# A scatter that adds: layer 1's expert results summed in device memory, residual rows stored ahead, last loads and stores on two queues

## The reference

```python
x = x + _L0_attn_ref(_layernorm(x), ...)
x = x + _L0_xattn_ref(_layernorm(x), ctx_2048, mask_BxS2_bk0)
x = x + _L0_ffn_ref(_layernorm(x), ...)
x = x + _L1_attn_ref(_layernorm(x), ...)
x = x + _L1_xattn_ref(_layernorm(x), ctx_2048, ctx_2048)
x = x + _L1_ffn_ref(_layernorm(x), ...)
```

```python
scores = jax.nn.softmax(jnp.einsum('bsh,eh->bse', x, router_w) + expert_bias, axis=-1)
top_w, top_idx = jax.lax.top_k(scores, 4)
top_w = top_w / jnp.sum(top_w, axis=-1, keepdims=True)
g = jnp.einsum('bsh,khe->bske', x, gate_proj)
u = jnp.einsum('bsh,khe->bske', x, up_proj)
out = jnp.einsum('bske,keh->bskh', jax.nn.silu(g) * u, down_proj)
sel = jnp.take_along_axis(out, top_idx[..., None], axis=2)
return jnp.sum(sel * top_w[..., None], axis=2)
```

## Time and profile before

| what | us |
|---|---|
| median of 3 runs | 970.37 (970.13 to 981.52) |
| the profiled execution | 980.05 |
| its span, first to last instruction | 978.1 |
| PE busy | 773.2 |
| DVE busy | 552.1 |
| ACT busy | 342.4 |
| POOL busy | 261.8 |
| first instruction of the last stage | 800.5 |
| last scatter of a block's result issued | 955.14 |

### The profile page before, as it was taken

How to read it: one execution, slowest core, us unless ns; L and a number is a source line. 1 busy time by engine, 2 the same in 40 slices (tenths; PEclk the granted TensorE clock), 3 DMA queues, 4 the chain that set the end, 5 groups by cost and what they waited for, 6 DMA issues and landing times. The chain is left out here.

```text
span 978.1 us, 13262 instructions
## 1 busy us (share of the span) xinstructions
PE 773.2 (79%) x4289; PEld 479.4 (49%) x4291; DVE 552.1 (56%) x1333; ACT 342.4 (35%) x781; POOL 261.8 (27%) x334
## 2 busy tenths in 40 slices
PE   4888844999999798994365899988987629999990
PEld 1454423788555465653123555555555315565550
DVE  4888944343232122224648999999986344455445
ACT  2455522333232122221333665666555202222220
POOL 2434314200000000003453334455331421333232
PEclk8999955999999999997566999999979659999995
DMA  9335504280077968663020001110130129999936
GB/s 350 159 157 215 215 1 150 81 318 17 5 274 274 360 221 293 239 236 99 13 63 1 9 15 35 34 47 26 47 135 25 49 85 330 319 325 319 328 117 225
DMA packets 52834, 151.90 MB, mean 155 GB/s; under 512 B 6720, under 2 KB 36288, under 8 KB 47648
## 3 DMA queue, kind: packets, MB, share of 16 engines
q1 hardware_dynamic: 47440, 135.99, 39.1%
q0 software_dynamic: 5328, 15.08, 4.2%
HBM read 109.87 MB, written 41.17 MB: 154 GB/s over the span
## 5 line engine op out<-in xcount | busy, mean ns | idle before, releaser
L1209 PE MATMUL ps<-f_rw,f_xT 128*128 128x512 f32 (+1 forms) x276 | 116.2, 545 | 17.1 <-DMA f_rw<-w_routed 16.5
L1130 DVE TENSOR_TENSOR f_rh<-f_gate,ps 128x256 f32<-128x256 f32 (+1 forms) x69 | 26.0, 377 | 142.8 <-ACT f_gate L1068 82.9
L2023 ACT ACTIVATE b_PX<-ps 128x512 f32<-128x512 f32 x128 | 72.9, 597 | 44.6 <-PE ps L2248 42.4
L1751 DVE TENSOR_REDUCE b_smax<-ps 128x4 f32<-128x1024 f32 x64 | 77.8, 1215 | 15.9 <-PE ps L2224 15.9
L1209 PEld LDWEIGHTS ps<-f_rw,f_xT 128*128 128x128 f32 x276 | 52.2, 194 | 50.4 <-issue 24.9
L2478 POOL DMA_INDIRECT y<-f_ys,f_to x47 | 45.1, 959 | 110.3 <-DVE f_ys L2527 109.3
L1068 ACT ACTIVATE f_gate<-ps 128x256 f32<-128x256 f32 (+1 forms) x69 | 24.0, 348 | 143.8 <-PE ps L1209 143.3
L1501 POOL MEMSET b_half<- 128x1 f32 x1 | 0.1, 98 | 273.6 <-POOLq L64 273.6
L2248 PE MATMUL ps<-b_Q,b_Cx 100*128 100x256 f32 x256 | 57.1, 328 | 10.6 <-ACT b_PX L2023 6.4
L1230 PE MATMUL ps<-f_rw,f_rhT 128*128 128x256 f32 x230 | 60.9, 380 | 0.5 <-ACT f_rhT L1054 0.5
L2224 PE MATMUL ps<-b_Cx,b_Q 96*128 96x512 f32 x128 | 47.5, 454 | 15.5 <-DVE b_smax L1751 9.6
(11 more groups left out here) (318 smaller groups left out, 1752.1 us busy)
## 6 DMA issues: line engine op xcount, KB each, us to landing
f_rw<-w_routed SPq DMA_DIRECT2D x23, 1920.0 KB, 8.0
rows<-a_blank SPq DMA_DIRECT2D x16, 1152.0 KB, 6.8
rw<-w_ffn SPq DMA_DIRECT2D x24, 704.0 KB
f_rw<-w_ffn SPq DMA_DIRECT2D x23, 704.0 KB
f_xs<-rows SPq DMA_DIRECT2D x47, 144.0 KB
f_yk<-y SPq DMA_DIRECT2D x8, 512.0 KB, 7.2
f_raw<-w_shared SPq DMA_DIRECT2D x10, 384.0 KB
b_Cx<-ctx_parts SPq DMA_DIRECT2D x96, 32.0 KB
```

What stands on the lines that cost most here:

```text
L1130: nc.vector.tensor_tensor(rh[u % 2][:, 0:n], gate[u % 2][:, 0:n], ps[:, u % 4, n:2 * n], ALU.mult).then_inc(r_h, 1)
L1209: mm = nc.tensor.matmul(ps[:, u % 4, 0:2 * n], xT[b % 2][:, c, :], rw[b % R_SLOTS][:, off:off + 2 * n], start=(c == 0), stop=(c == C - 1))
L1751: nc.vector.tensor_reduce(smax[t % 2][:, k // C, k % C, :], ps[:, FIRST:FIRST + 2, :].rearrange("p u (g n) -> p (u g) n", g=2), AX, ALU.ma ...
L2023: nc.scalar.activation(PX[g % RING][:].rearrange("p c m -> p (c m)"), ps[:, RETS + G_TURN[g] % 2, :], ACT.Exp, scale=XSC).then_inc(turn_re ...
```

## The change

`y1` is gone. In its place is `sums`, two sums of 1024 + 128 rows in device memory. Blocks with an even number add their rows to the first sum, those with an odd number to the second; the last 128 rows of each take the blank rows.

- In `attention0`, SP fills the rows from 1024 on with zeros (1.31 MB: the first sum's padding and the whole second sum), behind the clearing of `rows0` and ahead of the blank rows of `rows1`, and waits for it at the stage's end.
- In `attention1`, SP stores each tile of `X` into the first sum once `var_ready[2]` has counted it, behind the first weight loads. A row's address is now the token's number alone.
- In `sparse_experts`, the mask product and the reduction handle the weight only. The address comes straight from the loaded row, at most the padding row, plus 1152 for odd blocks; it is computed ahead of the reduction. POOL's scatter adds to what is in device memory. It waits, ahead of the scatter of block b, until that of b − 2, the one before it to the same sum, has landed.
- At the end, SP and ACT each wait for all scatters and load four tiles, 256 KB each with the two sums; DVE adds the two; SP and ACT each store the tiles they loaded. POOL has no part in it.

```diff
@@ attention0, SP
             sp.dma_start(rows_dram.rearrange("(b p) d -> p b d", p=P), bc(empty[:], 1, BLOCKS0)).then_inc(rows_cleared, 16)
+            sp.dma_start(sums_dram[TOKENS:2 * SUM_ROWS].rearrange("(b p) d -> p b d", p=P), bc(empty[:], 1, TILES + 2)
+                         ).then_inc(sums_cleared, 16)
...
             sp.wait_ge(rows_cleared, 16)
+            sp.wait_ge(sums_cleared, 16)
@@ attention1, SP
                 sp.dma_start(rw[n][:], w_ffn[n]).then_inc(w_loaded[n], 16)
+            for t in range(TILES):
+                sp.wait_ge(var_ready[2], t + 1)
+                sp.dma_start(sums_dram[t * P:(t + 1) * P], X[:, t, :]).then_inc(x_stored, 16)
+            sp.wait_ge(x_stored, 16 * TILES)
@@ attention1, DVE
-                nc.vector.tensor_scalar(row[s][:, D + E1:ROW1], rank[s][:], float(TOKENS), K[:, K_TOK + t:K_TOK + t + 1],
-                                        ALU.mult, ALU.add).then_inc(row_ready, 1)
+                nc.vector.tensor_copy(row[s][:, D + E1:ROW1], bc(K[:, K_TOK + t], 1, E1)).then_inc(row_ready, 1)
@@ sparse_experts
+        def take_sums(eng, q):
+
+            for n in range(Y_SLOTS):
+                eng.wait_ge(y_sent[n], 16 * ((BLOCKS1 + Y_SLOTS - 1 - n) // Y_SLOTS))
+            for t in range(q, TILES, 2):
+                eng.dma_start(yk[t][:], parts[t]).then_inc(yk_loaded[t], 16)
+
+        def store_sums(eng, q):
+
+            for t in range(q, TILES, 2):
+                eng.wait_ge(summed, t + 1)
+                eng.dma_start(out[:, t, :], X[:, t, :]).then_inc(stored[q], 16)
+            eng.wait_ge(stored[q], 16 * TILES // 2)
...
-                pool.indirect_dma_start(y_dram, bass.IndirectOffsetOnAxis(ap=to[b % A_SLOTS][:, 0:1], axis=0), ys[b % Y_SLOTS][:], None
-                                        ).then_inc(y_sent[b % Y_SLOTS], 16)
-            for t in range(1, TILES, 2):
-                pool.wait_ge(yk_loaded[t], 16)
-                nc.gpsimd.tensor_tensor(yk[t][:, 0:2], yk[t][:, 0:2], yk[t][:, 2:4], ALU.add).then_inc(odd_sum, 1)
+                if b >= 2:
+                    pool.wait_ge(y_sent[(b - 2) % Y_SLOTS], 16 * ((b - 2) // Y_SLOTS + 1))
+                pool.indirect_dma_start(sums_dram, bass.IndirectOffsetOnAxis(ap=to[b % A_SLOTS][:, 0:1], axis=0), ys[b % Y_SLOTS][:], None,
+                                        compute_op=ALU.add).then_inc(y_sent[b % Y_SLOTS], 16)
...
+                if b >= A_SLOTS:
+                    dve.wait_ge(y_sent[b % Y_SLOTS], 16 * (b // Y_SLOTS))
+                nc.vector.tensor_scalar(to[b % A_SLOTS][:], xs[b % X_SLOTS][:, D + E1:D + E1 + 1], K[:, K_PAD:K_PAD + 1],
+                                        float(b % 2 * SUM_ROWS), ALU.min, ALU.add).then_inc(to_ready, 1)
                 dve.wait_ge(aux_masked, b + 1)
...
+                dve.wait_ge(yk_loaded[t], 16)
+                nc.vector.tensor_tensor(X[:, t, :], yk[t][:, 0], yk[t][:, 1], ALU.add).then_inc(summed, 1)
```

More of the change, by code:

```diff
@@ L97, in decoder_kernel @@
 def decoder_kernel(nc, x, consts, routing, w_attn0, ctx_rows, ctx_cols, ctx_lhs, mask, w_shared0, w_routed0, w_attn1, lam, bias1, w_ffn1,
-                   out, ctx_dram, rows0_dram, y0_dram, rows1_dram, y1_dram):
+                   out, ctx_dram, rows0_dram, y0_dram, rows1_dram, sums_dram):
     with ExitStack() as whole:
@@ L1259, in routed_experts, with attention1 @@
     end_program(nc, semaphores)
-def attention1(nc, w_attn, ctx_lhs, lam, bias, X, K, KR, ps, ctx_dram, y_dram, y_dest, wk, rows_dram, w_ffn, rw, w_loaded, eb, rb, own):
+def attention1(nc, w_attn, ctx_lhs, lam, bias, X, K, KR, ps, ctx_dram, y_dram, y_dest, wk, rows_dram, w_ffn, rw, w_loaded, eb, rb, own,
+               sums_dram):
     ctx = ExitStack()
@@ L1445, in attention1 @@
         prefixed = sem("prefixed")
+        x_stored = sem("x_stored")
         counted = sem("counted")
@@ L2369, in attention1, with sparse_experts @@
     end_program(nc, semaphores)
-def sparse_experts(nc, tag, w_dram, rows_dram, y_dram, X, K, KR, ps, rw, w_loaded, eb, rb, own, out):
+def sparse_experts(nc, tag, w_dram, rows_dram, sums_dram, X, K, KR, ps, rw, w_loaded, eb, rb, own, out):
     ctx = ExitStack()
@@ L2394, in sparse_experts @@
         hT = [sb(f"hT{n}", [P, 2, P]) for n in range(2)]
-        aux = [sb(f"aux{n}", [P, 2, E1]) for n in range(2)]
-        pick = [sb(f"pick{n}", [P, 2]) for n in range(A_SLOTS)]
+        aux = [sb(f"aux{n}", [P, E1]) for n in range(2)]
+        pick = [sb(f"pick{n}", [P, 1]) for n in range(A_SLOTS)]
         to = [sb(f"to{n}", [P, 1], mybir.dt.int32) for n in range(A_SLOTS)]
         ys = [sb(f"ys{n}", [P, D]) for n in range(Y_SLOTS)]
-        nowhere = sb("nowhere", [P, BLOCKS1])
-        yk = [sb(f"yk{t}", [P, TOP1, D]) for t in range(TILES)]
+        yk = [sb(f"yk{t}", [P, 2, D]) for t in range(TILES)]
         xs_loaded = [sem(f"xs_loaded{n}") for n in range(X_SLOTS)]
         h_set = sem("h_set")
-        nowhere_set = sem("nowhere_set")
         x_turned = sem("x_turned")
@@ L2418, in sparse_experts @@
         yk_loaded = [sem(f"yk_loaded{t}") for t in range(TILES)]
[L2419 to L2423, removed]
+        summed = sem("summed")
+        stored = [sem(f"stored{n}") for n in range(2)]
         block = ctx.enter_context(nc.Block())
         ident = K[:, K_ID:K_ID + P]
+        parts = sums_dram.rearrange("(a t p) d -> t p a d", a=2, p=P)
+        def take_sums(eng, q):
[8 more added lines that the diff above has]
+            eng.wait_ge(stored[q], 16 * TILES // 2)
         @block.sync
@@ L2459, in _ @@
                 load_weights(b)
[L2460 to L2468, removed]
+            take_sums(sp, 0)
+            store_sums(sp, 0)
         @block.gpsimd
@@ L2517, in pick_own @@
                 nc.vector.tensor_reduce(pick[b % A_SLOTS][:], aux[b % 2][:], AX, ALU.add).then_inc(picked, 1)
[L2519 to L2523 removed]
             def keep_y(b):
                 dve.wait_ge(down_done, b + 1)
+                dve.wait_ge(picked, b + 1)
                 nc.vector.tensor_scalar(ys[b % Y_SLOTS][:], ps[:, 7, 0:D], pick[b % A_SLOTS][:, 0:1], None, ALU.mult).then_inc(y_kept, 1)
[L2529 to L2531 removed]
             dve.wait_ge(h_set, 1)
@@ L2541, in _ @@
                 pick_own(b)
-                address(b)
                 if b >= 2:
@@ L2707 @@
     rows1 = nc.dram_tensor("rows1", (SPARE1 + 1, P, ROW1), F32).ap()
-    y1 = nc.dram_tensor("y1", (TOP1 * TOKENS + BLOCKS1 * P, D), F32).ap()
-    decoder_kernel(nc, *args, out, ctx_parts, rows0, y0, rows1, y1)
+    sums = nc.dram_tensor("sums", (2 * SUM_ROWS, D), F32).ap()
+    decoder_kernel(nc, *args, out, ctx_parts, rows0, y0, rows1, sums)
     r = _run(nc, [arrays], core_ids=[0])
```

36 lines of the change are left out of this document (11 added, 25 removed).

## The result

| | before | changed |
|---|---|---|
| median of 4 runs, us | 972.75 (970.13 to 981.52) | 991.81 (987.09 to 993.38) |
| ratio, 95% interval | | 1.0172 [1.0095, 1.0249] |
| profiled execution, us | 980.05 | 991.02 |
| its span, us | 978.1 | 989.1 |

The account below looks back on a forecast made before the run. The scatter loop of the expert stage stood at the edge of PE's pace, with a serial end after it. Loop +11.9, last landing +0.4 and end −8.8 gave +3.5 us on 970.37, say 974 us; range 958 to 1012.

Parts of the forecast that it names:

- the rival of the second trip: Expert-stage scatter reads rows, waits, then writes: landing 6.9, block 4.28, together +39 us, 1010 us; chance 0.30.
- scatters 3.3 to 3.6 apart: Sign of being right: spacing in us of scatters in the loaded part of the expert stage.
- the 3.9 that was named as a sign of being wrong: Scatters over 3.9 us apart in the expert stage would show the forecast wrong.
- The loop: Expert-stage scatter loop: (5.2 + 1.66) / 2 = 3.43 us per block against 3.117, over 38 blocks +11.9 us.
- The landing: Adding scatter's time to land: +0.4 us for one more pass of the bytes, 5.2 loaded and 2.8 quiet.
- The turn: DVE between landing and next scatter: one reduction more, +0.25 us, from 1.41 to 1.66.
- POOL's wait: Scatter b behind the landing of b−2: adds nothing in the loop, cost 0 for block 46.
- The end: After the last scatter: halved loads and one add, 11.6 us against 20.4, −8.8 us; bounds −4 to −11.
- Clears and stores of X: First-stage clearing of 1.31 MB and eight stores of X: costed at nothing, with 15 us of room for the stores.
- The rule of two reads: Skill page: an adding transfer needs two source reads; engine time per scatter at most twice 0.37 us, sum stays +3.5.
- The add is hidden: Rival: loaded landing stays 4.82, only the turn costs, +4.7 − 8.8 = −4.1 us, 966 us; chance 0.20.
- for still more: Second-trip argument for a larger loss: PE busy falls to 70%; granted clock was 0.82 in 720 to 730.

Follow-up runs that it names:

- the control: The changed kernel as it is, run again on the chip of other follow-up kernels; 978.13 us, ratio to before 1.0148 [1.0113, 1.0183].

## Why the prediction was right, and which term was mis-sized

The direction and the stated range held: 991.8 lies inside 958 to 1012, and a ratio of 1.0172 is within 2%, the outcome that had 0.69, though its interval reaches past it. The mechanism, a landing that is paid for in the loop, was right. The size was not: the forecast's own range was 966 to 984, and the point, 974, was 18 us too low, of which 2.4 is the other median of the kernel before. The measured time lies between the forecast (landing 5.2) and the rival of the second trip (landing 6.9), and the range held because it was drawn to take in both. Of the prediction's own signs, the end (12.7 us, forecast 11 to 13) and f_to's wait (84.8 us, forecast some 30 and more) came out; scatters 3.3 to 3.6 apart and PE busy 87% did not (3.746 and 82%), and the control's 3.957 is past the 3.9 that was named as a sign of being wrong, for which the clock accounts.

- **The loop** as the bound, with landing plus turn over two: right. (6.05 + 1.44) / 2 is the measured 3.75 by its making; that the relation holds is shown by landings that are read one by one (the table above): 3.12 against 3.131 measured, and 3.67 against 3.745; and by the loop going to PE's pace once the landing is short or nobody on PE's path waits for it (2.991 and 2.995).
- **The landing, the term that failed.** I put the add at +0.4 us, "one more pass of the same bytes", 0.37 us of the engines. It was +1.23 in the loop and +1.29 in quiet (3.69 against 2.40). I had priced one more pass of the bytes and had no term for what the profile now shows: POOL is busy 0.59 longer with each scatter (1549 against 959 ns), and the rows go in three times as many packets, which take 0.56 us more of the engines (0.91 against 0.34). At 19 us per microsecond of landing the missing 0.83 is 16 us. The load beside it added nothing to this: 1.29 in quiet, 1.3 at the full pace of 2.99 us a block.
- **The turn** I put at +0.25 for the reduction behind the wait; it was +0.03. In the chain f_to takes 0.04 and f_pick 0.15 before f_ys, where f_to took 0.16 alone. DVE's timeline of the same turn shows why; the reduction starts at 833.67, before the address is done at 833.75:

```profile
833.54 0.21 DVE L2529 TENSOR_SCALAR f_to<-f_xs,K 128x1 int32<-128x1 f32 x1 [2.22 <-DMA sums<-f_ys,f_to]
833.67 0.16 DVE L2534 TENSOR_REDUCE f_pick<-f_aux 128x1 f32<-128x16 f32 x1
```

The error is 0.22 / 2 × 38 = −4 us and by luck hid part of the other.
- **POOL's wait** of b on b − 2: nothing in the loop, right (it shows once, 1.0 us, at the last scatter); it becomes the bound only with eight buffers. (The control's trace puts 9.6 us of POOL's waiting in its loop down to three landings. By the order of the code DVE had waited for the same landing before it wrote the result, so this is doubtful.)
- **The end**: −8.8 forecast, −7.7 measured. Issuing does not bound it, right: one queue or two makes no difference, and the transfer share is 0.97 from 977 to 986.
- **Clears and stores of X**: nothing, right. The stage before the experts took 345.9 us in the changed kernel, 338.5 in its control with the same code, 349.6 without the stores, and 349.4 before. The stores landed after 7.4 us in the median, not the 3.4 that was assumed, and the room was enough. The stages before that one, with the clears, ended at 445.91, against 451.09 before. SP's loads of rows wait for the address of block b − 10 now instead of its mask product, and so hang on landings too; that came to one wait of 0.5 us.
- **The rule of two reads.** The bound that the prediction drew from it was at most 0.37 us of the engines more per scatter; measured is 0.56 more, 0.91 against 0.34. The Trainium skill, page "Collectives: The Full Stack", section "The bandwidth ceiling: the fold count and why AG ≠ RS ≠ AR", gives that rule for the adding step of a ring between cores. For this scatter the trace does not agree with the bound drawn from it. Of the landing it said nothing, and there the cost was.
- **Rivals.** "The add is hidden" fell: it would be without the weight loads. "The second trip" came near: the loaded landing, 6.05, is the one from which this rival decides, but with the shorter turn the ratio came to 1.0172. Its price was 2.10 us per landing, and 1.29 was measured in quiet, so a full second trip is not what happens. The clock did not fall in the profiled execution. In the control's it did, as this rival's "for still more" had it: a mean of 0.93 with PE busy 125.66 of 151 us.

What stays open: how much of the 1.3 us is POOL's part and how much the transfers' themselves, with their smaller packets and the read that the add needs; no run here separates them.

## What to carry to other kernels

Moving a sum into the transfer saves bytes at the end, but here it made every scatter 1.3 us longer and added an order between them. Before doing so, look for who waits for a landing and what stands behind that wait; landing plus turn, divided by the number in flight, prices the loop in one line. Where memory allows, deepen buffers and the number of sums together: in this kernel neither alone was enough, and both together turned 1.5% slower into 0.7% faster. And give the kernel before the same buffers when you compare: with eight and no sums it was 0.4% faster too, which leaves the sums a gain that is not shown.

## What the runs showed of the hardware that was not expected

- A scatter of 128 rows of 1 KB that adds takes 144 packets where one that overwrites takes 48, and 0.91 against 0.34 us of all 16 engines; it keeps POOL busy 1549 against 959 ns, and lands in 3.69 against 2.40 us in quiet. Beside 330 GB/s of other traffic the landing is longer by the same 1.3 us (6.5 against 5.2).
- PE that had sat idle for 2.53 us behind a landing then ran a group of matmuls in 3.19 us that took 1.74 in the next block, in an execution with a mean granted clock of 0.93 in the loop; another execution of the same code had 1.00.
- A transfer share of 0.96 did not mean that the transfer engines were the limit: with three sums and eight buffers the share was 1.06 and PE ran at full pace; the same kind of block gave a share of 0.96 while 267 GB/s moved, and 1.06 while 330 moved.
- The attention stage of layer 1 takes 338.5 to 349.6 us in executions of the same or nearly the same code, with a mean granted clock between 0.86 and 0.82, as two windows of that stage show, of the control and of the changed kernel without the stores:

```profile
440.88:779.36 338.48, 243.09 (x1900) 145.36 (x1900) 270.22 (x580) 169.08 (x337) 145.90 (x182) 0.86 0.15 47
```

```profile
440.51:790.10 349.59, 253.07 (x1900) 150.28 (x1900) 270.49 (x580) 169.08 (x337) 145.97 (x183) 0.82 0.13 43
```

DVE and ACT are busy the same time in both; only PE's differs, by 10 us. So a difference of 1% between two single executions of this kernel says nothing; the ratio over several runs does, and the last stage by itself where its clock is the same.
